# A two-layer Flamingo-style block on one core: the choice of experts moved from a stage of its own into the first attention

## The reference, cut to what matters

```python
# x: (16, 256, 512) -> 4096 tokens of 512; ctx: (16, 256, 256)
x1 = x + tanh(g_xattn[0]) * cross_attention(layernorm(x), ctx)        # 16 heads of 128, first attention
# mixture of 8 experts, 2 a token:
h = layernorm(x1)
logits = (h * rsqrt(mean(h**2) + 1e-6)) @ router_logits * router_scale / sqrt(512)   # per token, 8 numbers
choose the two largest; share = softmax over those two; times per_expert_scale
x2 = x1 + tanh(g_ffn[0]) * sum over the two of share * expert(h)
# second attention (normed heads), then a feed-forward of 2048
```

## Time and profile before

| | us |
|---|---|
| median of 3 runs | 4042.14 |
| lowest and highest | 4035.44, 4044.68 |
| the profiled execution | 4030.16 |
| its span, first to last instruction | 4028.1 |
| TensorE busy in the span | 3645.7 (91%) |
| VectorE, ScalarE, GpSimd busy | 2286.1, 1844.9, 1495.8 |

### The profile page before, as it was taken

How to read it: one execution, slowest core, us unless ns; L and a number is a source line. 1 busy time by engine, 2 the same in 40 slices (tenths; PEclk the granted TensorE clock), 3 DMA queues, 4 the chain that set the end, 5 groups by cost and what they waited for, 6 DMA issues and landing times. The chain is left out here.

```text
span 4028.1 us, 69814 instructions
## 1 busy us (share of the span) xinstructions
PE 3645.7 (91%) x23284; PEld 3149.3 (78%) x23284; DVE 2286.1 (57%) x5901; ACT 1844.9 (46%) x4723; POOL 1495.8 (37%) x1580
## 2 busy tenths in 40 slices
PE   8999999999999964199999993999999869999999
PEld 7999999999999964199999982666666547777777
DVE  6666666656656662166666656888888542222221
ACT  4444445544444410155555541777777622222222
POOL 3333334433333313266666662555555520000000
PEclk9999999999999955599999996999999879999999
DMA  4112212211111141256666653111111030000000
GB/s 142 58 57 75 69 57 92 85 59 47 58 59 47 37 159 21 95 210 243 231 227 235 224 197 138 44 50 55 61 54 49 17 107 27 22 21 21 21 21 21
DMA packets 149252, 353.99 MB, mean 88 GB/s; under 512 B 18545, under 2 KB 35826, under 8 KB 144514
## 3 DMA queue, kind: packets, MB, share of 16 engines
q1 hardware_dynamic: 110610, 265.20, 19.3%
q10 hardware_dynamic: 23632, 45.16, 3.4%
q0 software_dynamic: 14880, 42.06, 2.8%
HBM read 271.72 MB, written 80.66 MB: 87 GB/s over the span
## 5 line engine op out<-in xcount | busy, mean ns | idle before, releaser
L539 POOL TENSOR_SCALAR a_prob<-a_prob,a_rinv 128x256 f32<-128x256 f32 x512 | 472.6, 935 | 869.9 <-DVE a_rinv L601 869.9
L502 ACT ACTIVATE a_prob<-a_prob,a_nbias 128x256 f32<-128x256 f32 x512 | 256.5, 502 | 427.5 <-DVE a_nbias L594 427.5
L1197 DVE TENSOR_TENSOR e_w_lo<-e_w_raw,e_w_hi 128x1024 fp32r<-128x1024 f32 (+1 forms) x316 | 330.5, 1087 | 60.6 <-ACT e_w_hi L1155 59.5
L1103 PE MATMUL e_gb<-e_xt_hi,e_w_hi 128*128 128x256 f32 x1248 | 356.0, 285 | 9.7 <-DVE e_xt_lo L1197 9.6
L1104 PE MATMUL e_gb<-e_xt_lo,e_w_hi 128*128 128x256 f32 x1248 | 354.8, 284 | 0.0
L1105 PE MATMUL e_gb<-e_xt_hi,e_w_lo 128*128 128x256 f32 x1248 | 354.8, 284 | 0.0
L2157 DVE TENSOR_TENSOR f_h_lo<-f_h_f,f_h_hi 128x512 fp32r<-128x512 f32 x128 | 92.1, 720 | 458.9 <-ACT f_h_hi L2133 458.9
L352 PE MATMUL a_pj<-a_xt,a_wq_hi 128*128 128x256 f32 x1024 | 310.2, 303 | 1.1 <-DVE a_q_lo L555 0.9
L2131 ACT ACTIVATE f_h_f<-f_hb,f_b_sb 128x512 f32<-128x512 f32 x128 | 88.2, 689 | 486.8 <-PE f_hb L2056 426.9
L354 PE MATMUL a_pj<-a_xt,a_wq_lo 128*128 128x256 f32 x1024 | 289.5, 283 | 0.0
L353 PE MATMUL a_pj<-a_xt,a_wq_hi 128*128 128x256 f32 x1024 | 289.1, 282 | 0.0
(11 more groups left out here) (362 smaller groups left out, 11436.3 us busy)
## 6 DMA issues: line engine op xcount, KB each, us to landing
e_w_raw<-in_w_gate SPq DMA_DIRECT2D x40, 2048.0 KB, 11.1
e_w_raw<-in_w_out SPq DMA_DIRECT2D x40, 1024.0 KB
xt_rows<-a_xt SPq DMA_DIRECT2D x16, 1024.0 KB, 4.8
a_xt<-xt_rows SPq DMA_DIRECT2D x16, 1024.0 KB, 4.9
d_y_sb<-y_rows SPq DMA_DIRECT2D x16, 1024.0 KB, 5.0
a_x_sb<-in_x SPq DMA_DIRECT2D x16, 512.0 KB, 5.6
a_ctx_raw<-in_ctx_t SPq DMA_DIRECT2D x32, 256.0 KB, 5.5
a_xr_sb<-in_x SPq DMA_DIRECT2D x16, 512.0 KB, 5.3
```

The source lines that it names most:

```text
L502: e = nc.scalar.activation(prob[:, u % 4, t], prob[:, u % 4, t], ACT.Exp, bias=nbias[:, u % 2, t:t + 1], scale=SCALE, accum_out=rsum[:, u ...
L539: p = nc.gpsimd.tensor_scalar(prob[:, u % 4, t], prob[:, u % 4, t], rinv[:, u % 2, t:t + 1], None, ALU.mult)
L1103: nc.tensor.matmul(out, a_hi, b_hi, start=start, stop=False)
L1197: return nc.vector.tensor_tensor(out, raw, hi.bitcast(F32), ALU.subtract)
```

## The change

`route` is gone as a stage. Its work is done inside the last 16 turns of the first attention, a batch (2 tiles) or a pair of batches (`QT` = 4 tiles) at a time, from the x1 rows that are still in `a_xo_sb`, with the attention's own PSUM banks and with buffers laid over ones that are no longer used (`xn`, `w_raw`, `x_sb`). New entries of `WHEN` place it: `rstat` (statistics, 13) and `rxn` (normalized rows, 14), the transposes `r0` and `r1` (16, 17), then per pair `lg` (logits, 18), `top` (19), `hot` (20), `share` (21), `rk` and `place` (27), and two indirect DMAs in each of `list0` to `list3` (28 to 31). The inverse roots are taken by GpSimd's power in place of Newton steps. The walk of the steps gets 19 more steps at the end, for what the last pair still needs. Six constants are loaded on SP ahead of the second half's weights; the empty lists are written at step 136. The first two pairs of the second half are written out, too, and the loop runs over five pairs in place of seven. The table is made as before.

```diff
--- before.py
+++ after.py
...
-def gated_cross_attention(nc, x_in, x_half, x_out, xt_rows, ctx_t, mask, gate, wq, wk, wv, wo, identity, tag):
+def gated_cross_attention_and_route(nc, x_in, x_half, x_out, xt_rows, xn_rows, slot_tokens, tile_table, weights, ctx_t, mask, gate, wq, wk, wv, wo,
+                                    logits_w, router_scale, expert_scale, gate_ffn, identity, earlier, iotas, pairs, empty_list, tag):
...
+    QT = 2 * S // P
+    STAT_LINKS, TOP_LINKS, SHARE_LINKS, PLACE_LINKS = 6, 5, 7, 5
...
+        blank, empty = w_raw[:, 2, 0:D], w_raw[:, 2, D:D + SLOTS // P].bitcast(I32)
+        xt1 = w_raw[:, 0:2].rearrange("p b (c s) -> p b c s", c=FC)
...
         WHEN = {"load_x": -11, "load_ctx": -11, "load_res": -2, "load_xt": -9, "keep_xt": -4, "stats": -9, "mask": -2, "xn": -7, "ctx": -8,
-                "x0": -6, "x1": -5, "k0": -4, "k1": -3, "v0": -2, "v1": -1, "out": 12}
+                "x0": -6, "x1": -5, "k0": -4, "k1": -3, "v0": -2, "v1": -1, "out": 12, "rstat": 13, "rxn": 14, "r0": 16, "r1": 17, "lg": 18, "top": 19, "hot": 20, "share": 21,
+                "rk": 27, "place": 27, "list0": 28, "list1": 29, "list2": 30, "list3": 31}
         SHARED = ("x0", "x1", "k0", "k1", "v0", "v1")
+        ROUTED = ("r0", "r1", "lg", "rk")
+        BY_PAIR = ("lg", "top", "hot", "share", "rk", "place", "list0", "list1", "list2", "list3")
         ONLY = {"load_x": (2, B), "load_ctx": (2, TURNS), "load_res": (1, TURNS), "load_xt": (B, TURNS), "keep_xt": (0, B),
                 "stats": (0, B), "xn": (0, B), "x0": (0, B), "x1": (0, B)}
         FIRST, AHEAD = -9, 5
-        LAST = TURNS * HEADS + 5
+        LAST = TURNS * HEADS + 24
 
         def live(n, what):
-            lo, hi = ONLY.get(what, (0, TURNS))
-            return lo <= n < hi
+            lo, hi = ONLY.get(what, (B, TURNS) if WHEN[what] > WHEN["out"] else (0, TURNS))
+            return lo <= n < hi and (n % 2 == 1 or what not in BY_PAIR)
...
-            with eng.Fori(half, 2 * half - 1) as i:
+            for n in (half, half + 1):
                 for u in range(AHEAD, AHEAD + PAIR):
-                    step((i, half, 2 * half - 2), u)
+                    step((n, n, n), u)
+            with eng.Fori(half + 2, 2 * half - 1) as i:
+                for u in range(AHEAD, AHEAD + PAIR):
+                    step((i, half + 2, 2 * half - 2), u)
...
+                for bb in due(f, u, "rxn"):
+                    sp.wait_ge(xn1_done, turn(f, bb, 1 - B))
+                    sp.nop(nofuse=True)
+                    sp.dma_start(xn_rows[rows(f, bb), :].rearrange("(t p) d -> p t d", p=P), x_sb[:, bb % 2]).then_inc(xn1_stored[bb % 2], 16)
...
+                    sp.wait_ge(pj_ready, number[B - 1, "x1"] + 1)
+                    for dst, src in ((before, earlier), (iota, iotas), (wr_raw, logits_w), (rscale, router_scale), (escale, expert_scale), (pair_no, pairs)):
+                        sp.dma_start(dst, src).then_inc(consts_loaded, 16)
...
+                if f[1] == f[2] and PAIR * f[1] + u == 136:
+                    low_done(sp, 2 * SET - 1)
+                    sp.dma_start(empty, empty_list).then_inc(empty_loaded, 16)
+                    sp.wait_ge(empty_loaded, 16)
+                    sp.dma_start(slot_tokens.rearrange("(p s) o -> p (s o)", p=P), empty).then_inc(cleared, 16)
+                    sp.wait_ge(blank_done, 1)
+                    sp.dma_start(xn_rows[TOK:TOK + P, :], blank).then_inc(cleared, 16)
...
+            def turn_x1(f, bb, j):
+                pe.wait_ge(xn1_done, turn(f, bb, 1 - B))
+                wait_room(f, bb, f"r{j}")
+                out = item_psum(f, bb, f"r{j}")
+                for c in range(2):
+                    for t in range(2):
+                        mm = nc.tensor.transpose(out[:, c, t * P:(t + 1) * P], x_sb[:, bb % 2, t, (2 * j + c) * P:(2 * j + c + 1) * P], ident[:])
+                mm.then_inc(pj_ready, 1)
+
+            def logits_of(f, bb):
+                pe.wait_ge(rt_done, at(f, lambda k: 2 * (2 * k + bb - B) + 2))
+                pe.wait_ge(wr_done, 1)
+                pe.wait_ge(ones_set, 1)
+                wait_room(f, bb, "lg")
+                out = item_psum(f, bb, "lg")
+                for t in range(QT):
+                    for c in range(FC):
+                        mm = nc.tensor.matmul(out[:, t], xt1[:, t // 2, c, t % 2 * P:(t % 2 + 1) * P], wr[:, c], start=(c == 0), stop=(c == FC - 1))
+                mm.then_inc(pj_ready, 1)
+
+            def ranks(f, bb):
+                pe.wait_ge(picked_done, pair_of(f, bb, 1))
+                wait_room(f, bb, "rk")
+                out = item_psum(f, bb, "rk")
+                nc.tensor.matmul(out, before[:], picked[:], start=True, stop=False)
+                for t in range(QT - 1):
+                    nc.tensor.matmul(out[:, t + 1:QT], ones[:], picked[:, t:t + 1].to_broadcast([P, QT - 1 - t, E]), start=False, stop=False)
+                mm = nc.tensor.matmul(out, ones[:], total[:].unsqueeze(1).to_broadcast([P, QT, E]), start=False, stop=True)
+                mm.then_inc(pj_ready, 1)
...
+            pe.wait_ge(pos_done, B // 2)
+            nc.tensor.matmul(ob[0][0:E, 0:1], total[:], ones[:, 0:1], start=True, stop=True).then_inc(number_ready, 1)
+            pe.wait_ge(tiles_done, 1)
+            nc.tensor.matmul(ob[0][:, E:2 * E], tiles_rep[0:E, :], upto[0:E, :], start=True, stop=True).then_inc(cum_ready, 1)
...
+                        act.wait_ge(pj_ready, made(f, bb, f"r{j}"))
+                        nc.scalar.copy(xt1[:, bb % 2, 2 * j:2 * j + 2], item_psum(f, bb, f"r{j}")).then_inc(rt_done, 1)
+                for bb in due(f, u, "hot"):
+                    act.wait_ge(gap_done, pair_of(f, bb, 1))
+                    nc.scalar.activation(odds[:], gap[:], ACT.Exp).then_inc(odds_done, 1)
...
+                    pool.wait_ge(rstat_link, at(f, lambda k: STAT_LINKS * (2 * k + bb - B + 1)))
+                    pool.nop(nofuse=True)
+                    nc.gpsimd.tensor_tensor(roots1[:, bb % 2], vars1[:, bb % 2], power[:], ALU.pow).then_inc(rroot_done, 1)
+                for t in range(QT):
+                    for bb in due(f, u, f"list{t}"):
+                        if t == 0:
+                            pool.wait_ge(cleared, 32)
+                            pool.wait_ge(pos_done, pair_of(f, bb, 1))
+                            pool.nop(nofuse=True)
+                        for k in range(TOPK):
+                            pool.indirect_dma_start(out=slot_tokens, out_offset=bass.IndirectOffsetOnAxis(ap=pos_here[:, t, k:k + 1], axis=0),
+                                                    in_=pair[:, t, k:k + 1], in_offset=None).then_inc(listed, 16)
+
             all_steps(pool, step)
+            pool.wait_ge(listed, 16 * QT * TOPK * (B // 2))
...
+            def rstat(f, bb):
+                done = [0]
+                then = chain(f, bb, rstat_link, lambda k: STAT_LINKS * (2 * k + bb - B), done)
+                dve.wait_ge(o_free, turn(f, bb, 3))
+                dve.nop(nofuse=True)
+                for t in range(2):
+                    op = V.bn_stats(stats[:, t], xo_sb[:, bb % 2, t])
+                then(op)
+                for t in range(2):
+                    op = V.bn_aggr(mv[:, t], stats[:, t])
+                then(op)
+                v = vars1[:, bb % 2]
+                then(V.tensor_scalar(v[:, 0:2], mv[:, :, 1], LN_EPS, None, ALU.add))
+                then(V.reciprocal(part[:], v[:, 0:2]))
+                then(V.tensor_tensor(part[:], part[:], mv[:, :, 1], ALU.mult))
+                V.tensor_scalar(v[:, 2:4], part[:], ROUTER_EPS, None, ALU.add).then_inc(rstat_link, 1)
+
+            def rxn(f, bb):
+                dve.wait_ge(rroot_done, turn(f, bb, 1 - B))
+                if not (f[1] == f[2] and 2 * f[1] + bb < B + 2):
+                    dve.wait_ge(xn1_stored[bb % 2], at(f, lambda k: 16 * ((2 * k + bb - B) // 2)))
+                    dve.wait_ge(rt_done, at(f, lambda k: 2 * (2 * k + bb - B) - 2))
+                    dve.nop(nofuse=True)
+                for t in range(2):
+                    op = V.tensor_scalar(x_sb[:, bb % 2, t], xo_sb[:, bb % 2, t], mv[:, t, 0:1], roots1[:, bb % 2, t:t + 1], ALU.subtract, ALU.mult)
+                op.then_inc(xn1_done, 1)
+
+            def top(f, bb, part_no, done):
+                then = chain(f, bb, top_link, lambda k: TOP_LINKS * ((2 * k + bb - B) // 2), done)
+                if part_no == 0:
+                    dve.wait_ge(pj_ready, made(f, bb, "lg"))
+                    dve.nop(nofuse=True)
+                    r2 = roots1[:, :, 2:4].unsqueeze(3).to_broadcast([P, 2, 2, E])
+                    op = V.tensor_tensor(logits[:].rearrange("p (b t) e -> p b t e", b=2), item_psum(f, bb, "lg").rearrange("p (b t) e -> p b t e", b=2), r2, ALU.mult)
+                    op.then_inc(lg_taken, 1)
+                    dve.wait_ge(lg_taken, pair_of(f, bb, 1))
+                    dve.nop(nofuse=True)
+                    for t in range(QT):
```

(51 more changed lines are left out.)

400 lines of the change are left out of this document (126 added, 274 removed).

## The result

| | before | changed |
|---|---|---|
| median, us | 4042.3 | 3952.7 |
| lowest and highest | 4035.4, 4044.7 | 3945.9, 3955.7 |
| span of the profiled execution | 4028.1 | 3953.2 |

The ratio is 0.9779, with a 95% interval of 0.976 to 0.9797: 90 us faster where 138 were forecast. By the profiled executions it is 74.9 us (that of before was 12 us shorter than its median). The forecast of 3904 was 49 us low; its range, to 3955, just holds the time.

The account below looks back on a forecast made before the run. TensorE, always busy at full clock in the attention, and the stage behind it bound the kernel: -247.1 + 43 (matmuls) + 17 (VectorE stalls) + 48.7 (tail) = -138.4 us, from the 4042.14 median to 3904; range 3868 to 3955.

Parts of the forecast that it names:

- What bounds the kernel: First attention: TensorE busy all the time at full clock, so added work costs its full price; other engines have room.
- The range: Whole kernel's time: 3868 us, lists' lower bound on the cheap case, up to 3955, past the dear case's middle.
- the dear rival: Attention and tail: lists in flight slow engines through 5.1 us waits and slow links; 15 to 75 us, middle 3945; chance 0.23.
- The removed stage: Between x1's last rows and the experts' first instruction: all 247.1 us go, as nothing else ran in them.
- The matmuls' prices: TensorE in the attention: logit 0.107 us, rank 0.11, four transposes 0.44; 4.5 a pair plus 0.88 a batch, 43 in all.
- Clock 1.00 until there: Sign in the new profile: TensorE's granted clock stays 1.00 until the last `out`, at about 1486 us.
- VectorE's burst: Attention steps 4 and 5: added VectorE work lags 5.1 us, TensorE stands 2.2; 2.5 a pair, 17 us in all.
- The slack of 2.9 us: Attention: from `a_ot_lo`'s end at 1023.31 to TensorE's next values at 1026.2, VectorE may lag 2.9 us without a stall.
- The tail: Behind the attention, in sequence: chain 22.3 us, eight list DMAs 19.8, barrier 6.6; 48.7 us to the experts.
- its chain: From x1's last rows to the first of the last lists: statistics, transposes, logits, `top`, `hot`, ranks, `place`, hand-overs; 22.3 us.
- Eight list DMAs at 2.48: Behind the attention: the last eight list DMAs cost 2.48 us each until landed, 19.8 us; bounds 10 to 25.
- only two DMAs are outstanding at a time, not sixteen: Argument against lists in flight slowing the attention: two outstanding there at a time, where the old stage's slow rows had sixteen.

Follow-up runs that it names:

- The kernel with 93.4 us a pair: Changed kernel with VectorE's new work cut into small pieces, logits spread, last pair's own buffers, and all 64 list DMAs behind the last place: ratio 0.9856.
- the even cut: Against the changed kernel: VectorE's new work in small pieces fitted to each step, logits spread, own buffers for the last pair; ratio 0.9704.
- the kernel with all lists last: Changed kernel with all positions kept in SBUF and all 64 list DMAs issued behind the last place, none inside the attention: ratio 0.9935.

## Why the prediction was right or wrong, point by point

**What bounds the kernel** was right: TensorE in the attention, and what it was given came back in the pair. The kernel with 93.4 us a pair is the sum of the old pair and the new matmuls, to within 0.7.

**The range** held the time by 2.3 us at its upper end, and that was luck. That end was set past the dear rival's middle of 3945, and the rival's mechanism, lists that slow the attention, added nothing to the six pairs here. What was missed lay elsewhere: in the clock, the last pair, the landing of the lists and the last `place`'s wait for them.

**The removed stage** was right, 247.1 us.

**The matmuls' prices** were right: 0.109 for a logit, 1.07 for a pair's ranks, 0.43 for four transposes, 6.3 a pair. "Clock 1.00 until there" was the first step that failed. The sum had no term for the clock; it cost 2.1 us a pair, 12 to 13 in six pairs, and more in the last turn, at 0.85 on average. The full clock of the stretch before was taken as given, when one of the added items was an unbroken 3.5 us of the smallest matmuls of the kernel. The Trainium skill, "TensorE: Matmul & The Clock Gate", section "Why this matters for your kernels", warns of idle gaps between bursts; here the clock fell with no gap, behind matmuls of 8 columns, so watching for gaps alone would have missed it.

**VectorE's burst** was right in place and nearly in size: 1.6 us behind it, forecast 2.2. The slack of 2.9 us was wrong. Its rows looked at `a_ot_lo`; the tile that TensorE met first was `a_pt_lo`, VectorE's first of a step, which TensorE's transposes at the end of that step need. So every step that is over-full by a few tenths of a microsecond shows, 0.3 to 0.8 us a time, also in steps that the forecast passed as covered. That is 3.3 us a pair in place of 2.5, 5 us in all. The moves of `hot` and `share`, each fitted to that slack, gained nothing; the even cut gained all.

**The attention's end** was not looked at by itself, and was the larger miss: the last pair took 87.8 us in place of 67.9, 19.9 more, where the forecast's share is 7.7. The steps there, from step 5 of turn 30 to the last head's scores, are 6.1, 6.1, 6.1, 5.1, 5.1, 8.2, 8.6, 4.7, 4.9 and 7.4; before, 6.1 three times, 4.7 six times and 3.3. That is 12.5 us more; the rest lies behind the last scores, where the clock was at half to 1505.5. The logits are there in full (the step of 8.2). ScalarE's stand falls into the step behind them, the 8.6. These two took 16.8 us together, and 15.3 in the kernel with all lists last, which has no such stand, so it is worth some 1.5 us; TensorE's own wait for it is 2.0 (`a_sc` above). And there are no keys or values in the last turn, so that VectorE's `out`, `hot`, `rstat` and `share` fall into two steps of 4.7 with no room for them; TensorE waits 3.2 us for the `a_pt_lo` behind them, the longest wait of all:

```profile
1493.05 1.09 PE L502 MATMUL a_ptb<-a_ident,a_prob 128*128 128x128 f32 x4 [3.18 <-DVE a_pt_lo L710]
```

The forecast's prices were means over seven equal pairs. Six pairs at 2.9 over the forecast, 12.2 more in the last and 2.6 before the first make up the 32.6 us to within 0.4.

**The tail** was right in its chain: 33.1 us to the first list (1518.6 to 1551.7), of which 10.6 are the wait, so 22.5 for a forecast of 22.3. Two steps failed. "Eight list DMAs at 2.48" turned a fixed time into a price a piece: 39.7 us for sixteen was 19.0 of issue and 20.7 of landing, and eight are 8.9 and the same landing. The three numbers stood in the text, and the division hid them; a second count was needed to tell them apart. This is 8.6 us, first list to experts 35.0 for 26.4. And `place` reads no new data but writes over `pos_here`, so it waits for the eight before it; in the loop these are twelve steps old, in the drain they have just been issued. The prediction didn't price that wait: 10.6 us.

The Trainium skill, "DMA: Bandwidth & Descriptors", section "Anatomy of one DMA — SWDGE (gpsimd) path", gives a fixed 2.0 us. The trace disagrees by ten times: 21 us from the last issue to the wait's end at L816. The issue at 1.26 us each, from the earlier trace rows, did hold.

**The dear rival** had a middle of 3945, near the time, but not by its mechanism, which was harmless in this schedule: by their place the lists cost the six pairs nothing (97.9 without them, 98.1 with). It was ruinous with the lists four steps earlier: 109.2, and 99.8 with ranks and places just as early but no list. There its single long waits near the jump back came true (9.3 us and more against 2.7; the loop jumps back four times, not five); its ground against, "only two DMAs are outstanding at a time, not sixteen", was wrong, since with some 20 us to land and one issued every 2 to 3 us all eight are outstanding together.

**Open.** What an engine waits for in such a stand is in no row. That its next code is late is a reading that fits VectorE at the jump back (2.7 without lists, 9.3 and more with), ScalarE in straight code, and the same stretch's late transfers; it was only argued, and moving the jump away from the lists left pairs of 98.9 to 108.4. Why 128 entries of 4 bytes hold other transfers and take 20 us to land was not tried either. The Trainium skill, "DMA: Bandwidth & Descriptors", section "Specifications", says that pieces under 512 bytes are read, changed and written back; no run here shows that as the cause.
